# A three-layer cross network over 16 blocks: the first steps of the pipeline in another order

## The reference

```
out = relu(einsum('bfd,bgd,fgs->bsd', x, h, Wr) + b)     # Wr = W.reshape(39, Fk, 128)
if i != 2: h, direct = out[:, :64], out[:, 64:]
else:      direct = out
```

## Time and profile before

| what | value |
|---|---|
| median of 3 runs | 584.98 us (584.91 to 585.09) |
| the profiled execution, its own time | 584.89 us |
| its span in the profile | 583.1 us |
| PE, DVE, ACT, POOL busy | 559.0, 536.2, 374.3, 514.0 us |
| granted TensorE clock, mean | 0.984 of full |

### The profile page before, as it was taken

The page is one execution under the profiler, slowest core; times in us unless marked ns, Lnnn a source line. Parts: engine busy times, 40 slices in busy tenths (PEclk is TensorE's granted clock), DMA queues, the critical chain, the costliest instruction groups (busy, mean ns, idle before and its releaser), DMA issues.

```text
span 583.1 us, 7873 instructions
## 1 busy us (share of the span) xinstructions
PE 559.0 (96%) x2029; PEld 383.8 (66%) x2029; DVE 536.2 (92%) x514; ACT 374.3 (64%) x419; POOL 514.0 (88%) x229
## 2 busy tenths in 40 slices
PE   3895999999999999999999999999999999999997
PEld 1363676767666676776666677676666767667765
DVE  3588989999999999999999999999999999999975
ACT  2476556576757667665766766666586676758562
POOL 0687959989898998989999898998989899898995
PEclk9796999999999999999999999999999999999999
DMA  8999734927558383755828366582846649162001
GB/s 332 420 417 346 276 109 118 346 78 269 215 166 325 98 324 118 245 223 177 327 79 318 142 218 250 158 343 68 308 166 191 277 139 348 65 215 97 0 2 37
DMA packets 26959, 121.69 MB, mean 209 GB/s; under 512 B 3264, under 2 KB 3392, under 8 KB 24768
## 3 DMA queue, kind: packets, MB, share of 16 engines
q1 hardware_dynamic: 26944, 121.52, 57.4%
HBM read 120.98 MB, written 0.52 MB: 208 GB/s over the span
## 4 chain that ended last, share of the span: by engine, by line
PE 86%; issue 4%; DMA 3%; DVE 3%; POOL 2%; ACT 2%; SPq 0%; POOLq 0%; DVEq 0%; ACTq 0%
PE acc L471 86%; DMA xfirst<-x 3%; POOL z_lo L234 2%; DVE z_raw L351 1%; DVE z_whole L351 1%; ACT z_hi L540 1%; ACT h L543 0%; ACT last L543 0%; DVE z_hi L232 0%; DVE z_psum L351 0%; DVE z_lo L234 0%; SPq L244 0%; ACT direct L543 0%; DVE sums L374 0%; DVE z_lo L231 0%
## 5 line engine op out<-in xcount | busy, mean ns | idle before, releaser
L234 POOL TENSOR_TENSOR z_lo<-z_raw,z_hi 128x1024 fp32r<-128x1024 f32 (+1 forms) x222 | 508.1, 2325 | 49.1 <-ACT z_hi L540 46.9
L540 ACT CAST z_hi<-z_raw 128x1024 fp32r<-128x1024 f32 (+1 forms) x222 | 223.4, 1019 | 116.3 <-DVE z_raw L351 83.7
L351 DVE TENSOR_TENSOR z_raw<-h,xwide 128x1024 f32<-128x1024 f32 x192 | 229.8, 1219 | 8.5 <-ACT h L543 7.4
L471 PE MATMUL acc<-z_hi,w_hi 128*128 128x512 f32 (+2 forms) x557 | 219.3, 463 | 7.7 <-ACT direct L543 6.9
L471 PE MATMUL acc<-z_hi,w_lo 128*128 128x512 f32 (+2 forms) x557 | 181.7, 396 | 0.0
L471 PE MATMUL acc<-z_lo,w_hi 128*128 128x512 f32 (+1 forms) x525 | 169.8, 397 | 1.3 <-POOL z_lo L234 1.1
L471 PEld LDWEIGHTS acc<-z_hi,w_hi 128*128 128x128 f32 (+2 forms) x557 | 105.1, 189 | 67.5 <-issue 40.0
L471 PE MATMUL acc<-z_whole,w_whole 128*128 128x512 f32 x256 | 124.6, 611 | 2.8 <-DVE z_whole L351 2.8
L471 PEld LDWEIGHTS acc<-z_hi,w_lo 128*128 128x128 f32 (+2 forms) x557 | 104.8, 188 | 28.2 <-issue 3.6
L471 PEld LDWEIGHTS acc<-z_lo,w_hi 128*128 128x128 f32 (+1 forms) x525 | 98.2, 188 | 27.4 <-POOL z_lo L234 3.3
L351 DVE TENSOR_TENSOR z_whole<-h,xwide 128x1024 f32<-128x1024 f32 x64 | 77.8, 1217 | 5.3 <-ACT h L543 5.3
(11 more groups left out here) (16 smaller groups left out, 91.4 us busy)
## 6 DMA issues: line engine op xcount, KB each, us to landing
xwide<-x SPq DMA_DIRECT2D x160, 512.0 KB, 4.7
xfirst<-x SPq DMA_DIRECT2D x15, 2048.0 KB, 7.7
xwide<-w SPq DMA_DIRECT2D x2, 1024.0 KB, 12.6
xfirst<-x SPq DMA_DIRECT2D x2, 768.0 KB, 6.0
xfirst<-x SPq DMA_DIRECT2D x1, 512.0 KB, 6.9
w_whole<-w_rest SPq DMA_DIRECT2D x1, 512.0 KB, 10.3
w<-w0a SPq DMA_DIRECT2D x1, 448.0 KB, 5.1
direct<-w0b SPq DMA_DIRECT2D x1, 448.0 KB, 6.1
```

Of the source, the lines that this page charges most:

```text
L234: return eng.tensor_tensor(lo[0:rows, 0:n, :], z[0:rows, 0:n, :], hi[0:rows, 0:n, :].bitcast(F32), ALU.subtract)
L351: nc.vector.tensor_tensor(dst, in0, in1, ALU.mult).then_inc(made[kind], 1)
L471: return nc.tensor.matmul(dst, w[0:rows, place, :], z[0:rows, t - G * g, :], start=first and first_g and t == G * g, stop=final and t == T ...
L540: nc.scalar.copy(z_hi[0:rows, slot("PV", pair, par, pos, HI_RING), 0:n, :], src).then_inc(hi_made, 1)
```

## The change

Step -1 gets block 0's first layer as before, and step 0 opens with block 1's first layer, all whole, and then has block 0's second layer in the order 1, 3, 0, 2, 6, 4, 7, 5, 8, 9, of which 1, 3, 0, 2, 6, 7 are whole (before: 1 and 3); the weights of the four that are split in later blocks are read by PE from `stage[1]`. Step 1 opens with block 2's first layer. Block 1's first tile lands in a place of its own (half 1 of `xwide`); for blocks 0 and 1 xrep is read in SBUF. w0 is loaded and folded in two parts. On ACT relu0 of block 0 moves ahead of the split of w1, xrep's copy for block 2 stands at the end of step 0, and the split of w2 and DVE's low part of it stand in step 1, at places 6 and 7. SP's order changes with them. The main parts:

```diff
-FIRST_0 = (1, 3, 0, 2)
-SCHEDULE_0 = "111100001111112222222222"
-SCHEDULE_1 = "111222222211000011111222"
-RELU1_AT_1 = 3
+ORDER_1_0 = ((1, "W"), (3, "W"), (0, "W"), (2, "W"), (6, "W"), (4, "P"), (7, "W"), (5, "P"), (8, "P"), (9, "V"))
+SCHEDULE_1 = "000011111211222211212222"
+RELU1_AT_1 = 4
+SPLIT2_AT_1, LOW2_AT_1 = 6, 7
...
-         0: [(1, g, KINDS[1][g]) for g in FIRST_0] + steps(SCHEDULE_0)[len(FIRST_0):],
+         0: [(0, g, "W") for g in range(len(KINDS[0]))] + [(1, g, k) for g, k in ORDER_1_0],
...
+        xsecond = xwide[:, 1, 0:1 + T0, :]
...
-            load_first(0, xfirst_head_in[0], range(0, 1 + G))
-            sp.dma_start(w0[:], w0a).then_inc(w0_in, 16)
-            sp.dma_start(w0t, w0b).then_inc(w0_in, 16)
+            for k, ts in enumerate(FOLD):
+                sp.dma_start(w0[:, ts[0]:ts[-1] + 1, :], w0a[:, ts[0]:ts[-1] + 1, :]).then_inc(w0_in[k], 16)
+                sp.dma_start(w0t[:, ts[0]:ts[-1] + 1, :], w0b[:, ts[0]:ts[-1] + 1, :]).then_inc(w0_in[k], 16)
+                if k == 0:
+                    load_first(0, xfirst_head_in[0], range(0, 1 + G))
             load_first(0, xfirst_head_in[1], range(1 + G, 1 + 2 * G))
             sp.dma_start(bias[:], b).then_inc(bias_in, 16)
             load_first(0, xfirst_in, range(1 + 2 * G, 1 + T0))
+            load_first(1, xsecond_in[0], range(0, 1 + G), xsecond)
+            load_first(1, xsecond_in[1], range(1 + G, 1 + T0), xsecond)
+            load_wide(0, 0, ORDER_1_0[0][0])
+            sp.dma_start(w_whole[:], w_rest).then_inc(w_whole_in, 16)
+            load_wide(0, 0, ORDER_1_0[1][0])
             sp.dma_start(stage[1][:, 0:SPLIT_COUNT[1], :], w1).then_inc(w_staged[1], 16)
-            sp.dma_start(w_whole[:], w_rest).then_inc(w_whole_in, 16)
-            for g in FIRST_0:
+            for g, _ in ORDER_1_0[2:]:
                 load_wide(0, 0, g)
             sp.wait_ge(*made_all(-1, 0))
-            load_first(1, xfirst_in)
-            for g in range(4, 6):
-                load_wide(0, 0, g)
+            load_first(2, xfirst_in)
+            sp.wait_ge(*made_all(0, 0))
+            for g in range(2):
+                load_wide(1, 1, g)
             sp.dma_start(stage[2][:, 0:SPLIT_COUNT[2], :], w2).then_inc(w_staged[2], 16)
-            for g in range(6, G12):
-                load_wide(0, 0, g)
-            for g in range(G12 - 4):
+            for g in range(2, G12 - 4):
                 load_wide(1, 1, g)
-            sp.wait_ge(*made_all(0, 0))
-            load_first(2, xfirst_in)
             sp.wait_ge(w1_lo_made, 1)
+            sp.wait_ge(whole_used, before("W", 1, 0))
+            for g in range(G12 - 2, G12):
+                load_wide(1, 1, g)
             sp.wait_ge(w2_lo_made, 1)
-            for g in range(G12 - 4, G12):
+            for g in range(G12 - 4, G12 - 2):
...
+                        dve.wait_ge(xrep_ready, j)
+                        dve.wait_ge(xfirst_in, 16 * (j + 1))
+                    if isinstance(j, int) and j < 1:
+                        tile = xfirst if j < 0 else xsecond
+                        in0 = tile[0:P0, 0:1, :].to_broadcast([P0, n, N])
+                        in1 = tile[0:P0, 1 + G * g:1 + G * g + n, :]
+                    else:
+                        in0 = xrep_psum[0:P0, None, :].to_broadcast([P0, n, N])
+                        in1 = xshift[:, G * g:G * g + n, :]
...
+                    if isinstance(j, int) and j == 1 and pos == LOW2_AT_1:
+                        a, n = SPLIT_FROM[2], SPLIT_COUNT[2]
+                        dve.wait_ge(w_hi_made, len(SPLIT0) + 2)
+                        nc.vector.tensor_tensor(w_lo[:, a:a + n, :], stage[2][:, 0:n, :],
+                                                w_hi[:, a:a + n, :].bitcast(F32), ALU.subtract).then_inc(w2_lo_made, 1)
...
+            def fold(k):
+                ts = FOLD[k]
+                dve.wait_ge(w0_in[k], 32)
+                part = w0[:, ts[0]:ts[-1] + 1, :]
+                nc.vector.tensor_tensor(part, part, w0t[:, ts[0]:ts[-1] + 1, :], ALU.add).then_inc(w0_folded, 1)
+            fold(0)
             products(-1, 0, 0)
-            dve.wait_ge(w0_in, 32)
-            nc.vector.tensor_tensor(w0[:], w0[:], w0t, ALU.add).then_inc(w0_folded, 1)
+            fold(1)
             for pos in range(1, len(order(-1))):
                 products(-1, 0, pos)
             step(-1, 1)
-            a, n = SPLIT_FROM[2], SPLIT_COUNT[2]
-            dve.wait_ge(w_hi_made, len(SPLIT0) + 2)
-            nc.vector.tensor_tensor(w_lo[:, a:a + n, :], stage[2][:, 0:n, :], w_hi[:, a:a + n, :].bitcast(F32),
-                                    ALU.subtract).then_inc(w2_lo_made, 1)
...
+                    w = w0 if layer == 0 else w_whole
+                    if layer and KINDS[layer][g] != "W":
+                        pe.wait_ge(w_staged[1], 16)
+                        w = stage[1]
                     for t in ts:
-                        mm = matmul(w0 if layer == 0 else w_whole, z, t, True, True)
+                        mm = matmul(w, z, t, True, True)
...
             pe.wait_ge(w0_folded, 1)
-            step(-1, 0)
+            contract(-1, 0, 0)
+            pe.wait_ge(w0_folded, 2)
+            for pos in range(1, len(order(-1))):
+                contract(-1, 0, pos)
...
-                    if isinstance(j, int) and j == 0 and (layer, g) == SPLIT2_BEFORE:
+                    if isinstance(j, int) and j == 1 and pos == SPLIT2_AT_1:
                         split_layer(2)
                     if kind != "W":
                         high_part(pair, par, pos)
                 if isinstance(j, int) and j == 0:
+                    copy_xrep(1)
...
-            copy_xrep(-1)
-            act.wait_ge(w0_folded, 1)
+            act.wait_ge(w0_folded, 2)
             for a, ts in SPLIT0:
                 split(w0[0:P0, ts[0]:ts[-1] + 1, :], a, len(ts), P0)
-            split_layer(1)
             act.wait_ge(bias_in, 16)
             relu0(-1, 0)
+            split_layer(1)
```

More of the change, by code:

```diff
@@ L129 @@
 SPLIT0 = [(PLACE[0, tiles_of(0, g)[0]], tiles_of(0, g)) for g, k in enumerate(KINDS[0]) if k != "W"]
-SPLIT2_BEFORE = (1, 6)
+FOLD = (range(0, G), range(G, T0))
+assert sorted(g for g, _ in ORDER_1_0) == list(range(G12))
 assert len(SPLIT0) > 0 and SPLIT_COUNT[1] <= 16 and SPLIT_COUNT[2] <= 16
@@ L170, in cin @@
                  xwide[:, 1, T12 - 8:T12 - 4, :].rearrange("p a (b s) -> p (a b) s", s=SIZE)]
+        xsecond = xwide[:, 1, 0:1 + T0, :]
         w0t = direct[:].rearrange("p a (b s) -> p (a b) s", s=SIZE)[:, 0:T0, :]
-        w0_in = sem("w0_in")
+        w0_in = [sem("w0_in0"), sem("w0_in1")]
         w0_folded = sem("w0_folded")
@@ L183, in cin @@
         xfirst_head_in = [sem("xfirst_head_in0"), sem("xfirst_head_in1")]
+        xsecond_in = [sem("xsecond_in0"), sem("xsecond_in1")]
         xw_in = [[sem(f"xw_in{p}_{g}") for g in range(G12)] for p in range(2)]
@@ L240, in _, with load_first @@
         def _(sp):
-            def load_first(j, landed, slots=range(1 + T0)):
+            def load_first(j, landed, slots=range(1 + T0), tile=xfirst):
                 src = bass.AP(x0.tensor, x0.offset + 128 * (1 + T0) * N * j + N * slots[0],
                               [[(1 + T0) * N, 128], [1, len(slots) * N]])
-                sp.dma_start(xfirst[:, slots[0]:slots[-1] + 1, :], src).then_inc(landed, 16)
+                sp.dma_start(tile[:, slots[0]:slots[-1] + 1, :], src).then_inc(landed, 16)
             def load_wide(j, half, g):
@@ L314, in products @@
                 if layer == 0:
-                    if g == 0:
-                        dve.wait_ge(xrep_ready, j + 2)
                     if isinstance(j, int) and j == -1:
@@ L322, in products @@
                             dve.wait_ge(xfirst_in, 16)
+                    elif isinstance(j, int) and j == 0:
+                        if g < len(xsecond_in):
+                            dve.wait_ge(xsecond_in[g], 16)
                     elif g == 0:
-                        dve.wait_ge(xfirst_in, 16 * (j + 2))
-                    in0 = xrep_psum[0:P0, None, :].to_broadcast([P0, n, N])
-                    in1 = xshift[:, G * g:G * g + n, :]
+                        dve.wait_ge(xrep_ready, j)
[7 more added lines that the diff above has]
+                        in1 = xshift[:, G * g:G * g + n, :]
                 elif layer == 1:
@@ L469, in matmul @@
                     rows = rows_of(layer, t)
-                    place = t if w is w0 else PLACE[layer, t]
+                    place = t if w is w0 else PLACE[layer, t] - (SPLIT_FROM[1] if w is stage[1] else 0)
                     return nc.tensor.matmul(dst, w[0:rows, place, :], z[0:rows, t - G * g, :],
@@ L482, in contract @@
                     z = z_whole[:, slot("W", pair, par, pos, WHOLE_RING)]
+                    w = w0 if layer == 0 else w_whole
+                    if layer and KINDS[layer][g] != "W":
+                        pe.wait_ge(w_staged[1], 16)
+                        w = stage[1]
```

(21 more changed lines are left out.)

## The result

The changed kernel takes 577.74 us (median of 4 runs, 577.21 to 578.90) against 584.94 (4 runs): 0.9881 of it, 95% interval 0.9863 to 0.9898. Forecast were 577.0, in a range of 571.8 to 581.5. The profiled execution took 578.0 us, its span is 576.0; before they were 584.89 and 583.1.

What follows compares the result with a forecast made beforehand. DMA, then ACT, DVE and POOL were taken to bound step 1, PE only waiting. From 584.89 us, 7.3 for opening step 2 earlier and 0.63 for two waits gave 576.9, with the median's 0.09 577.0; range 571.8 to 581.5.

Steps and rivals of the forecast that it cites:

- The yardstick: The moment PE opens step 2: 87.94 us before, forecast 80.6 us, 7.3 us earlier.
- The second term: In step 2, PE's two waits for POOL's low parts go, 0.63 us.
- PE isn't the bound up to step 0: PE ends step 0 at 39.5 to 42.7 us, against 44.0 before, and does not set the time there.
- The chain: Step 1: from xrep's copy after block 2's DMA at 37.8 us, ACT, DVE and POOL set step 2's opening at 80.6.
- the landing of block 2's tile: Ahead of step 1, block 2's x for the first layer lands by DMA at 37.8 us.
- PE's waits in step 1: Between places 4 and 18, PE waits several times for POOL's low parts, 4 to 5 us in all.
- the exclusion: DVE's subtraction for w2's low part and POOL's SBUF-reading instructions exclude each other; 2.14 us remain after POOL, ending at 50.85.
- the bound without contention: In step 1, w2's low part on DVE ends at 50.3 us if POOL does not hold it up.
- PE as the bound: Rival, 12%: PE's own work sets step 1, step 2 opens at 75.5, time 571.8 us.
- low clock in step 1: Rival, 3%: PE's stops in step 1 bring and keep 1.2 GHz, 15 us more, 592 us.
- The pause at the seam: Rival, 2%: PE's second stop moves to the seam of steps 0 and 1, 585 us, no change.

Runs made afterwards that it cites:

- x8: Changed kernel with block 1's first layer summed in h1's bank, so PE doesn't pause between the two first layers: 577.52 us.
- the second execution: The changed kernel run again with no edit, as the mark for other runs on its chip: 578.11 us median, profiled execution 577.14 us.
- x4: Changed kernel with DVE making w2's low part ahead of place 9 of step 1 instead of place 7: 576.57 us.
- x1: Changed kernel with only groups 1 and 3 whole in block 0's second layer, the other eight split, new group order kept: 579.16 us.
- x5: Changed kernel with step 1 in its old order, opening with block 1's second layer, and w2 loaded and split early: 579.02 us.
- y4: Changed kernel with relu1, w2's split and low part at places 5, 8, 9, w0 in one piece, w1/w2 staging exchanged, block 1's first layer summed in h1's bank: 575.60 us.
- y1: Changed kernel with step 1's relu1 before place 5, w2's split before place 8, its low part before place 9: 577.72 us.

## Why the prediction was right

- **The yardstick.** Step 2 opened 6.17 us earlier, and what follows is shorter by 496.95 - 496.23 = 0.72: 6.9 us, as the times say. The second term was priced at 0.63. (The group that opens step 2 is block 2's group 0 of the second layer; the prediction calls it block 1's.)
- **PE isn't the bound up to step 0.** Right in what follows from it, and shown by x8. The numbers for PE were too early: I had it through with step 0 at 39.5 to 42.7, measured 43.53. It started at 9.00 instead of 7.4 (8.07 in the second execution), and the pause ended at 20.02, not 17.9: the first layer ended later, and I overlooked a wait that I could have read in the code, `w_whole_in` ahead of step 0, for w_rest, which landed at 20.02, behind relu0's end at 19.79.
- **The chain.** Forecast from the copy to step 2: 80.6 - 37.8 = 42.8 us; measured 42.80, and 42.76 to 42.80 in the second execution and in four kernels more. Its largest terms: w2's high part done at 49.12 - 38.97 = 10.15 behind the copy (48.2 - 37.8 = 10.4 forecast), the low part at 12.97 (13.05), POOL's eight on end from 16.4 (16.6), step 2 7.41 behind PE's pass with the last of them (7.3). None is off by over 0.3, so the sum isn't right by luck.
- **The mis-sized term is the landing of block 2's tile**: 37.8 forecast, 38.97 in the profile, 38.16 in the next execution. The 0.3 us for two small DMAs at the head of the queue were too little. With w0 in one piece the copy stands at 37.74 to 37.80 (and where it waits longest, 2.62 us, at 37.75), 0.2 to 0.3 us behind the 37.5 that the rate of 404 KB/us gives, so the rate was right, and four pieces instead of two cost 0.4 to 1.2 us. This is all of the 1.2 us by which step 2 missed 80.6.
- **PE's waits in step 1**: 2.79 us with the fifth, forecast 4 to 5. Same cause as above: PE came later. Had PE come at 40, as in x8, it would have waited 4.8 in step 0 and 1 together.
- **Shared access**: the exclusion held, on both sides, with the sum as forecast. The 2.14 us that I took for the subtraction's own time are what is left of it behind POOL's end (2.15 measured); alone it takes 2.28 (x4), so the bound without contention was 0.14 too low. Nothing hung on it.
- **Rivals.** PE as the bound fell with x8 and x1. No low clock in step 1: it was 1.00 from 27 us on in spite of five waits of up to 0.97. The pause at the seam didn't come back.
- **One reason was incomplete.** I put the 6.90 us down to the seam and didn't say which of relu1's effects PE waited for. x5 shows it: the accumulator of the second layer, not h. Nor did I say why relu1 was so late: the low part of w2 stood ahead of step 1's first products on DVE, and moving it behind them is a part of the change that the prediction priced in the new kernel only.

## What to carry to other kernels

When four engines feed one another, find the arrival that comes last and price the queues behind it to the end of the stage; a pause or a low clock of the busiest engine ahead of that point can be worth nothing (x8) until the chain beside it is cut (y4). What another order takes off a seam may be earned a step later, where the cover changes (x5). When an operation is moved, count the loads that stand behind its wait in the DMA-issuing queue (x4, y1).
